# Column sums of the weights times beta moved from VectorE to TensorE, the decay tile built later, and the unit matrix loaded by itself

## The reference, cut to what matters

```
xn  = layernorm(x)
s   = recurrent layer of xn:
        a second layernorm with gamma, beta
        u = xn' @ W_in + b_in               (2048 -> 8)
        h = scan(u, sigmoid(decay_logit))   (along the sequence)
        x1 = xn + h @ W_out + b_out + xn' * D_skip
        hf = relu(layernorm(x1) @ W_down + b_down)      (2048 -> 32)
        s  = x1 + hf @ W_up + b_up
y   = fake_quant(relu(fake_quant(xn) @ fake_quant(kernel) + fake_quant(bias)))   (2048 -> 2048)
out = x + s * silu(y)
```

## Time and profile before

| | us |
|---|---|
| median of 3 runs (lowest, highest) | 605.12 (605.01, 605.27) |
| the profiled execution, own time | 605.74 |
| its span on the slowest core (core 7) | 604.2 |
| spans of the 8 cores | 600.9 to 604.2 |
| PE busy in the span | 553.4 (92%) |
| DVE, ACT, POOL busy | 510.8, 518.8, 443.8 |

### The profile page before, as it was taken

The page is one execution under the profiler, slowest core; times in us unless marked ns, Lnnn a source line. Parts: engine busy times, 40 slices in busy tenths (PEclk is TensorE's granted clock), DMA queues, the critical chain, the costliest instruction groups (busy, mean ns, idle before and its releaser), DMA issues.

```text
span 604.2 us, 10061 instructions; the slowest of 8 cores (600.9 to 604.2 us)
## 1 busy us (share of the span) xinstructions
PE 553.4 (92%) x3538; PEld 272.1 (45%) x3538; DVE 510.8 (85%) x1181; ACT 518.8 (86%) x497; POOL 443.8 (73%) x709
## 2 busy tenths in 40 slices
PE   0367987999999999999999999999999999999993
PEld 0355643444444444444444444444444444444441
DVE  3899978888888888888898888889888888899755
ACT  2858988998888888988888999888888988888864
POOL 2568767777777787777778777777788777778840
PEclk9768899999999999999999999999999999999997
DMA  8999653767777676777767766877667778798513
GB/s 240 335 347 312 220 132 68 190 201 205 209 196 198 200 190 178 195 205 209 182 183 194 199 194 200 209 197 206 195 178 202 182 201 209 191 191 183 132 71 140
DMA packets 141683, 118.89 MB, mean 197 GB/s; under 512 B 130368, under 2 KB 130368, under 8 KB 131520
## 3 DMA queue, kind: packets, MB, share of 16 engines
q1 hardware_dynamic: 141632, 118.24, 71.1%
HBM read 52.17 MB, written 33.55 MB: 142 GB/s over the span
## 4 chain that ended last, share of the span: by engine, by line
PE 84%; ACT 6%; DVE 5%; DMA 2%; issue 1%; POOL 1%; SPq 0%; ACTq 0%; DVEq 0%; POOLq 0%
PE py L519 71%; PE pu L570 3%; PE px L646 3%; DMA x<-L_attn_x 2%; PE px L578 2%; DVE kst L333 1%; PE px L367 1%; PE px L608 1%; ACT xc L474 1%; DVE t L441 1%; PE pt L637 1%; ACT junk L350 1%; ACT zix L490 1%; ACT kq L389 1%; ACT k L350 1%
## 5 line engine op out<-in xcount | busy, mean ns | idle before, releaser
L519 PE MATMUL py<-kq,ixT 128*128 128x512 bf16 x2048 | 462.9, 380 | 3.6 <-ACT py L501 3.2
L519 PEld LDWEIGHTS py<-kq,ixT 128*128 128x128 bf16 x2048 | 194.3, 98 | 228.2 <-ACT py L501 12.9
L658 POOL TENSOR_TENSOR x<-x,g 128x512 f32<-128x512 f32 x124 | 155.1, 1272 | 56.6 <-DVE g L653 54.2
L615 ACT ACTIVATE junk<-px 128x2048 bf16<-128x2048 f32 x32 | 60.1, 1877 | 49.5 <-PE px L608 49.5
L527 DVE CUSTOM_DVE_ANT_0 t<-py,sc_bc,st 128x512 f32<-128x512 f32 x96 | 71.5, 745 | 21.7 <-PE py L519 21.6
L501 ACT ACTIVATE py<-brow,st 128x512 f32<-128x512 f32 x128 | 86.6, 677 | 3.8 <-DVE st L527 2.9
L441 DVE BATCH_NORM_STATS2 t<-x 128x6 f32<-128x512 f32 x128 | 81.5, 681 | 2.8 <-DMA x<-L_attn_x 2.8
L653 DVE TENSOR_TENSOR g<-px,g 128x512 f32<-128x512 f32 x124 | 77.0, 683 | 0.5 <-ACT g L542 0.5
L481 DVE TENSOR_REDUCE st<-xc 128x1 f32<-128x2048 f32 x32 | 72.8, 2275 | 2.2 <-ACT xc L474 2.2
L465 POOL TENSOR_SCALAR zix<-xc,ln 128x2048 bf16<-128x2048 f32 x32 | 65.4, 2045 | 3.7
L474 ACT ACTIVATE xc<-x,st 128x2048 f32<-128x2048 f32 x32 | 63.7, 1992 | 3.4 <-DVE st L447 3.4
(11 more groups left out here) (162 smaller groups left out, 608.5 us busy)
## 6 DMA issues: line engine op xcount, KB each, us to landing
x<-L_attn_x SPq DMA_DIRECT2D x32, 1024.0 KB, 5.6
out<-x SPq DMA_DIRECT2D x31, 1024.0 KB, 4.3
x<-L_ffn_kernelT SPq DMA_DIRECT2D x7, 1024.0 KB, 10.3
g<-L_ffn_kernelT SPq DMA_DIRECT2D x3, 1024.0 KB, 16.0
t<-L_ffn_kernelT SPq DMA_DIRECT2D x2, 1024.0 KB, 15.8
xc<-L_ffn_kernelT SPq DMA_DIRECT2D x2, 1024.0 KB, 16.7
spare<-L_ffn_kernelT SPq DMA_DIRECT2D x2, 1024.0 KB, 17.3
out<-x SPq DMA_DIRECT2D x4, 256.0 KB, 2.0
```

What stands on the lines that cost most here:

```text
L519: P.put(lambda e, j=j: e.matmul(bank[:], ixT[c % 2][:, 128 * j:128 * (j + 1)], kq[:, D * j + 512 * q:D * j + 512 * (q + 1)], start=False, ...
L658: G.put(lambda e: e.tensor_tensor(x_t[c % 4][:, 512 * q:512 * (q + 1)], x_t[c % 4][:, 512 * q:512 * (q + 1)], g_t[:, 512 * q:512 * (q + 1) ...
```

## The change

1. The DVE sum `v_bws` (L293) is gone, with its tile. `p_sums` instead runs 16 f32 products, one per 128 features, that accumulate in the same 40 columns of `py`.
2. The tile of decays (`v_decay`, 4 instructions) moves on DVE from behind slab 4 to behind the last `k_rows`, just before `v_amax(1)`.
3. The unit matrix is loaded alone (64 KB) in the place where all constants were; the other 448 KB come behind the first rows of x. The copies `eye16` and `eyeb` wait for the first of them.
4. `bias_numbers` (one maximum on DVE, one transpose on PE) moves behind the maximum of slab 2.

```diff
-        def v_bws():
-            V.put(lambda e: e.tensor_reduce(bws[:], bw[:].rearrange("p (j r) -> p r j", r=40), AX, OP.add), "bw", mark="bws")
-
         def p_sums():
...
-            P.put(lambda e: e.matmul(py[0][:, 0:40], onesf[:], bws[:], start=True, stop=True, skip_group_check=True), "bws",
-                  mark="c40_mm")
+            for j in range(ND):
+                P.put(lambda e, j=j: e.matmul(py[0][:, 0:40], onesf[:], bw3[:, j, :], start=(j == 0), stop=(j == ND - 1),
+                                              skip_group_check=True), "bw", mark="c40_mm" if j == ND - 1 else None)
...
-        Y.dma(lambda e: e.dma_start(out=cst[:], in_=dcst), d_c, mark="consts")
+        Y.dma(lambda e: e.dma_start(out=eyef, in_=dcst[:, 0:128]), d_e, mark="eye")
         load_x(0)
+        Y.dma(lambda e: e.dma_start(out=cst[:, 128:1024], in_=dcst[:, 128:1024]), d_c, mark="consts")
...
         step(0)
-        bias_numbers()
         v_stats(0, 0)
...
         scaled(2)
+        bias_numbers()
         back(0, V)
...
         step(4, 4)
-        v_bws()
-        v_decay()
         bias_scaled()
...
         turn_z(1)
+        v_decay()
         v_amax(1)
```

More of the change, by code:

```diff
@@ L157, in build_nc @@
         gsum = sb("gsum", [128, 32], F32)
-        bws = sb("bws", [128, 40], F32)
         hfS = sb("hfS", [128, 128], F32)
@@ L183, in build_nc @@
         d_c = semaphore("d_const")
+        d_e = semaphore("d_eye")
         d_b = semaphore("d_big")
@@ L227, in g_eyes @@
         def g_eyes():
-            G.put(lambda e: e.tensor_copy(eye16[:], eyef), "consts", mark="eye16")
+            G.put(lambda e: e.tensor_copy(eye16[:], eyef), "eye", mark="eye16")
             G.put(lambda e: e.tensor_copy(eyeb[:], eyef), mark="eyeb")
```

## The result

The changed kernel takes 607.52 us (median of 6 runs, 607.18 to 607.91); the kernel before, on the same chip, 605.27. The ratio is 1.0036, with a 95% interval of 1.0022 to 1.005: slower, by 0.2 to 0.5%. The forecast was 607.0. Some executions fall into a slower state (one of six of the kernel before, at 705.09 us), and all times and ratios here are of the others.

What follows compares the result with a forecast made beforehand. PE was taken to bound 600 us, untouched by the change, with the early chain running through DVE, then PE and ACT. Loads 0, decay 0, products +1.9 and P to U unchanged gave 607.0 us, range 603.4 to 608.4.

Steps and rivals of the forecast that it cites:

- The products: Sixteen f32 products on PE ahead of the turn of `z0`: 6.9 us at clock 0.50, moving `p_half(0, 0)` by +1.9 us.
- P: Start of the first 16 products of `p_half(0, 0)`; forecast at 52.5 instead of 50.68 on core 7.
- The sum: Whole kernel: loads 0, decay 0, products +1.9, P to U unchanged; median 605.1 becomes 607.0 us.
- U: Transpose of `uS`, the last product before the steady part; whatever moves it on the latest core moves the time by as much.
- The clock: PE under the sixteen products: granted clock stays at 0.50 throughout; 52%, for 606.4 to 607.8 us.
- Rival A: PE's clock rises under the sixteen products: 603.4 us if at 39.7, 604.4 to 605.1 if later; 27%.
- The cost of a pass: Each f32 product on PE is two passes of 0.21 us at clock 0.50, against the skill page's 33 ns.
- Rival B: The f32 passes on PE follow each other as bf16 ones do, 0.9 us in all: 601.1 us; 6%.
- The loads: Start of the kernel: x about 1.5 us earlier, but DVE then waits for slab 2; value 0, bounds 0 and +0.4.
- The decay tile: Four DVE instructions, 1.7 us, moved into an idle 1.38 us before `v_amax(1)`; value 0, bounds 0 and +0.3.
- P to U: Stretch from `p_half(0, 0)` to the transpose of `uS`: stays 34.96 us, as a late core meets the low clock.
- Rivals C and D: C: late cores keep clock 1.00 after P, 605.7 us, 8%. D: low clock lasts into `p_half(0, 0)`, 608.7 us, 7%.

Runs made afterwards that it cites:

- e3: The kernel before with only the sixteen f32 products in place of DVE's sum; decay tile and loads as before: 607.67 us, ratio 1.0039.
- e6: The changed kernel with the sum taken twice, 32 f32 products instead of 16: 614.41 us, ratio 1.0145 to the kernel before.
- e8: The changed kernel with nine bf16 products of 512 columns added in PE's pauses between slabs 2 and 4: 605.54 us, ratio 0.9996 to the kernel before.
- e12: The changed kernel with its sixteen f32 products behind the turn of `z0` instead of ahead of it: 607.90 us, ratio 1.0031 to the kernel before.
- e7: The changed kernel with 40 columns in the first product and 8 in the fifteen others: 607.52 us, ratio 1.0034 to the kernel before.
- e2: The changed kernel with `bw` and the ones in bf16, so the sixteen products are bf16: 602.45 us, ratio 0.9951 to the kernel before.
- e4: The kernel before with only the split load of the constants and the later `bias_numbers`: 605.42 us, ratio 1.0001.
- e5: The kernel before with only the decay tile built later, just before `v_amax(1)`: 605.08 us, ratio 0.9991.
- e10: The changed kernel with DVE's sum and one f32 product back, and the bias numbers ahead of that sum: 603.20 us, ratio 0.9963 to the kernel before.

## Why the prediction was right

**The products: right, and this is the whole effect.** 6.9 us were forecast, 6.83 measured; `z0` at 45.0 (45.04), slab 6 at 47.8 (47.95), P at 52.5 (52.66). e3 has the loss with nothing else changed. A further sixteen cost the full 6.9 us (e6), since nothing is left to cover them.

**The sum: right on the latest core, with the median 0.5 us above it.** U is 87.44 on the latest core for 85.64, 1.8 us later against 1.9 forecast. Over the eight cores U moved by 2.6 us on the mean (83.76 to 86.36), because the late cores got their wait for the bank of `py` back (slab 6 to P: up to 5.71 us before, 4.71 now) and the early ones had none. The median rose by 2.2, between the two.

**The clock: the right choice for a reason only half seen.** I took 0.50 because one stretch with f32 transposes had not raised the clock. The runs are plainer: it stayed there through 13.4 us of such passes (e6). But it also depends on what PE did ahead of them: behind added bf16 products (e8) or behind the turn of `z0` (e12) they ran at 1.00 on five and on four cores of eight, and on core 5 of e12 it fell under them although PE was busy without a pause. Rival A, 27%, came about on no core of the changed kernel, where all eight took 0.213 us a pass. The Trainium skill, page "TensorE: Matmul & The Clock Gate", section "What's actually happening", says that activity releases the throttle. On core 5 of the changed kernel the clock did rise, under the turn of slab 5; under 13.4 us of f32 passes in e6, with PE shown busy throughout, it did not.

**The cost of a pass: right against the page.** By the gap of 33 ns for 40 columns that the Trainium skill gives, same page, section "Back-to-back issue gap", the passes would have been over in an estimated 1.1 us. In f32 they take 0.213 us at the low clock, with 40 columns as with 8 (e7), and 0.112 at the high one (e8); in bf16 the rule and the row agree (0.033). Rival B, 601.1, has the mechanism of e2 (602.45), with the cheap passes made rather than found.

**The loads: 0, right.** DVE waits 2.02 us for slab 2 in place of x; e4 shows no change. The statistics of x came 1.2 us earlier on the mean of the eight cores (14.8 for 16.0), where 1.5 were forecast.

**The decay tile: its own size was wrong, its effect on this sum nothing.** 1.7 us was the time at the old place, part of which was waiting for POOL. At the old place L290 took 1.29 to 1.74 us; at the new one it takes 0.6 (core 2 of e2) and all four fit into the pause. Nothing of this shows beside a DVE that waits 5.5 us, but it would have misled me if the products had been cheap: e5 gives 0.5 us, not 1.7.

**P to U: right.** Core 5 has 34.78 for the 34.96 I took. I had counted three of the four latest cores before with the low clock after P; the trace has it on all four (0, 2, 3 and 7). In the changed kernel it is there on four again, the four with the latest U (0, 3, 5 and 7). Rivals C and D did not occur: the late cores met the low clock after P, and the sixteen products at P took 3.63 us on all eight cores.

Beyond the two kernels, e2 is the fastest (602.45), at the price of bf16 in these sums; with f32 kept, e10 (603.20).

## What to carry to other kernels

Price an instruction moved to another engine in the type it has there: sixteen f32 products with a stationary operand of 128 x 128 cost 6.8 us at the granted clock 0.50, in place of 1.4 us of DVE, while the same in bf16 cost 0.5. Ask which engines stand in line behind the new work, not how busy the receiving engine is. And where DVE and POOL both work on SBUF, a short DVE instruction may hide a wait for POOL: removing it hands the wait to the next one, so look at when POOL's instruction ends before counting a duration as work. Where the column of the clock has shown no change yet, read the clock from the length of an instruction whose two lengths you know.

## What the runs showed of the hardware that I had not expected

- An f32 product whose stationary operand is 128 x 128 is two passes of 0.213 us at the granted clock 0.50, whether 8 or 40 columns are streamed, and of 0.112 at 1.00 with 40.
- Under such passes the granted clock stayed at 0.50 for 13.4 us (e6). It fell from 1.00 to 0.50 under them on three cores of e8, and at 41.6 on core 5 of e12, where PE had had no pause since 34.85.
- The profile's clock reads 1.00 from the start of the span until its first recorded change, also on cores whose passes take 0.213 us.
- A TENSOR_TENSOR of one column on DVE took 1.63 us instead of 0.16, and a TENSOR_SCALAR of 16 columns 1.85 instead of 0.23, both ending with a POOL instruction; TENSOR_REDUCE beside the same one kept its 1.39.
